# Splitting the two layer-norm loops of a transformer-layer kernel into halves one tile apart

## The chip, the cores and the metric

The kernel is one launch on the 8 cores of a Trainium2 chip. Every core runs the same program on its own data and no core waits for another. The metric is the device time of the slowest core, in microseconds (us). Each core has a matrix engine (TensorE, PE in the profile), a vector engine (VectorE, DVE), an activation engine (ScalarE, ACT), a general engine (GpSimd, POOL) and SyncE (SP). SP and POOL here mostly issue DMA transfers. Each engine works through its own instructions in order, and semaphores tie the engines together.

## The reference, cut to what matters

The input x has the shape (4, 2048, 2048). One layer is an attention block and a feed-forward block, each ahead of it a layer norm over the last axis and each added to its input:

```python
def _layernorm(x, axis=-1, eps=1e-5):
    m = jnp.mean(x, axis=axis, keepdims=True)
    v = jnp.var(x, axis=axis, keepdims=True)
    return (x - m) / jnp.sqrt(v + eps)

x = x + attn(_layernorm(x), ...)   # latent K/V, rotary part, 16 heads, causal, output projection
x = x + ffn(_layernorm(x), ...)    # silu(x gate * s) * (x up * s), then down * s; fp8 weights
```

Only the two `_layernorm` calls and the transposes behind them are touched by the change.

## The kernel before, in words

Two cores share one of the four sequences; each has all 2048 rows of it for keys and values and is answerable for 1024 rows of output. The stages follow one another, each closed by `kb.barrier()`, which makes every engine wait for all semaphores: first layer norm, latent projection, Q projection, attention in two groups of 8 heads, output projection with the residual written to the scratch tensor `res_scr`, second layer norm, gate and up, down.

The first layer norm runs over 16 tiles of 128 rows by 2048 values, the second over 8. Both have the same form. SP loads tile `it` (1 MB, float32) into `XT[it % 2]`, one half of the buffer `F32A`; there are two such halves. The load of tile `it` waits on SP until `lnct[it - 2]`, the normalisation of the tile that was in that half. Then `ln_tile` does the following. ACT sums the row (L242). DVE squares it and sums the squares (`scalar_tensor_tensor`, L244). Four DVE instructions on one column each make mean and variance (L247 to L250). ACT takes the square root (L252). DVE takes the reciprocal (L256) and writes the normalised tile in bf16 into `XHB` (L257). `vedge` is a DVE instruction followed by DVE's own wait for it, since the next instruction reads its result. The small values stand in `STAT`, 8 columns, used anew by every tile.

PE then transposes the 16 blocks of 128 by 128 in two halves (`tp_group`, L191), and DVE copies each half from PSUM into `BIG0` or `BIG1` (L197). The order on DVE is therefore: squares and small instructions of a tile, its reciprocal and normalisation, its two copies, and then the next tile. The order on ACT is: sum of a tile, its square root, sum of the next tile. The order is written out by hand: every engine's list is filled as the Python loops emit it.

The x load is L264, its wait comes two lines before it; the load of the second layer norm is L687. Behind the first stage POOL issues the load of the weights `wkvaT` (L208), behind the second that of `gatew` and `upw` (L721, L723).

Of the kernel before, what the change touches and what calls it, by code (L numbers as in the profile page):

```python
# [9 lines left out]
F32 = mybir.dt.float32  # L10
BF16 = mybir.dt.bfloat16
FP8 = mybir.dt.float8e4
AFT = mybir.ActivationFunctionType
# [80 lines left out]
def build_nc():  # L94
# [34 lines left out]
    res_d = nc.dram_tensor("res_scr", [1024, 2048], F32, kind="Internal")  # L129
# [4 lines left out]
    sb = lambda n, sh, dt: es.enter_context(nc.sbuf_tensor(n, sh, dt))  # L134
    pt = lambda n, sh, dt: es.enter_context(nc.psum_tensor(n, sh, dt))

    BIG0 = sb("BIG0", [128, 32768], BF16)
    BIG1 = sb("BIG1", [128, 16384], BF16)
    BIG2 = sb("BIG2", [128, 16384], BF16)
    LATT = sb("LATT", [128, 8192], BF16)  # L140
    XHB = sb("XHB", [128, 4096], BF16)
    WT = sb("WT", [128, 4096], BF16)
    PB = sb("PB", [128, 1024], BF16)
    SQB = sb("SQB", [128, 2048], BF16)
# [21 lines left out]
    BIASC = sb("BIASC", [128, 32], F32)  # L166
    BNS = sb("BNS", [128, 24], F32)
    AGG = sb("AGG", [128, 16], F32)
    STAT = sb("STAT", [128, 8], F32)
    KC = sb("KC", [128, 16], F32)  # L170
    MAXQ = sb("MAXQ", [128, 1], F32)
    MAXK = sb("MAXK", [128, 1], F32)
# [4 lines left out]
    EPSC = sb("EPSC", [128, 2], F32)  # L177

    PS = [pt(f"PS{i}", [128, 512], F32) for i in range(6)]
    PT = [pt("PT0", [128, 1024], BF16), pt("PT1", [128, 1024], BF16)]  # L180

    kb = KB(nc)
# [3 lines left out]
    A = bass.AP  # L186

    def tp_group(src, n, pti, dst, src_f32=False):
        kb.wait("tensor", "sV", kb.pt_ev[pti])
        for j in range(n):  # L190
            tct = kb.op("tensor", lambda e, j=j: e.matmul(  # L191
                PT[pti][:, j * 128:(j + 1) * 128], src[:, j * 128:(j + 1) * 128], IDB[:, :],
                is_transpose=True, start=(j == 0), stop=(j == n - 1)),
                inc="sT" if j == n - 1 else None)
        kb.wait("vector", "sT", tct)
        out_ap, in_ap = dst(n)
        ev = kb.op("vector", lambda e, o=out_ap, i=in_ap: e.tensor_copy(o, i), inc="sV")  # L197
        kb.pt_ev[pti] = ev
        return ev
# [11 lines left out]
    try:  # L211
# [4 lines left out]
        for dst0, src0 in consts:  # L216
            cload = kb.dma("sync", lambda e, d=dst0, s=src0: e.dma_start(
                out=d[:, :], in_=s.ap()[:, :]))
# [15 lines left out]
        XT = [F32A[:, 0:2048], F32A[:, 2048:4096]]  # L234

        def vedge(fn):
            v = kb.op("vector", fn, inc="sV")
            kb.wait("vector", "sV", v)
            return v

        def ln_tile(buf, xh, eps_col):
            s_sum = kb.op("scalar", lambda e, buf=buf: e.activation(  # L242
                BIG2[:, 0:2048], buf, AFT.Identity, accum_out=STAT[:, 0:1]), inc="sS")
            vedge(lambda e, buf=buf: e.scalar_tensor_tensor(  # L244
                SQB[:, 0:2048], buf, 1.0, buf, Op.mult, Op.mult, accum_out=STAT[:, 1:2]))
            kb.wait("vector", "sS", s_sum)
            vedge(lambda e: e.tensor_scalar(STAT[:, 2:3], STAT[:, 0:1], 1.0 / 2048, None, Op.mult))  # L247
            vedge(lambda e: e.tensor_scalar(STAT[:, 4:5], STAT[:, 1:2], 1.0 / 2048, None, Op.mult))
            vedge(lambda e: e.tensor_mul(STAT[:, 3:4], STAT[:, 2:3], STAT[:, 2:3]))
            v_var = kb.op("vector", lambda e: e.tensor_sub(STAT[:, 5:6], STAT[:, 4:5], STAT[:, 3:4]), inc="sV")  # L250
            kb.wait("scalar", "sV", v_var)
            s_sd = kb.op("scalar", lambda e, eps_col=eps_col: e.activation(  # L252
                STAT[:, 6:7], STAT[:, 5:6], AFT.Sqrt, bias=EPSC[:, eps_col:eps_col + 1],
                scale=1.0), inc="sS")
            kb.wait("vector", "sS", s_sd)
            vedge(lambda e: e.reciprocal(STAT[:, 7:8], STAT[:, 6:7]))  # L256
            return kb.op("vector", lambda e, xh=xh, buf=buf: e.tensor_scalar(  # L257
                xh, buf, STAT[:, 2:3], STAT[:, 7:8], Op.subtract, Op.mult), inc="sV")

        lnct, evA = {}, {}  # L260
        for it in range(16):
            if it >= 2:
                kb.wait("sync", "sV", lnct[it - 2])
            ld = kb.dma("sync", lambda e, it=it: e.dma_start(  # L264
                out=XT[it % 2], in_=xb.ap()[it * 128:(it + 1) * 128, :]))
            kb.wait("vector", *ld)
            kb.wait("scalar", *ld)
            xh = XHB[:, (it % 2) * 2048:(it % 2) * 2048 + 2048]
            if it >= 2:
                kb.wait("vector", "sT", evA[it - 2])  # L270
            lnct[it] = ln_tile(XT[it % 2], xh, 0)
            kb.wait("tensor", "sV", lnct[it])
            for half in range(2):
                src = xh[:, half * 1024:half * 1024 + 1024]
                dst = lambda n, half=half, it=it, pti=half: (
                    A(BIG0, half * 8 * 2048 + it * 128, [[32768, 128], [2048, 8], [1, 128]]),
                    PT[half][:, 0:1024])
                evA[it] = tp_group(src, 8, half, dst)
            evA[it] = kb.cnt["sT"]
        kb.barrier()  # L280

        cut(2)
# [20 lines left out]
        for dl in range(4):  # L303
# [5 lines left out]
            for tb in range(4):  # L309
# [26 lines left out]
                if pending is not None:  # L336
# [5 lines left out]
                                                      bias=EPSC[:, 1:2], scale=1.0 / 512), inc="sS")  # L342
# [66 lines left out]
        for hg in range(2):  # L409
            k_ev = {}  # L410
            mm_k = {}
            for i8 in range(8):
# [7 lines left out]
                for tb in range(4):  # L420
                    for c in range(4):
# [4 lines left out]
                            inc="sT" if (tb == 3 and c == 3) else None)  # L426
# [8 lines left out]
            for i8 in range(8):  # L435
# [37 lines left out]
                out=A(XHB, 0, [[4096, 128], [1024, 4], [1, 1024]]), in_=vin))  # L473
            kb.wait("tensor", *wv_ld)
            v_ev = {}
            for tt in range(16):
# [3 lines left out]
                for dl in range(4):  # L480
                    for ovb in range(2):
# [4 lines left out]
                            inc="sT" if (dl == 3 and ovb == 1) else None)  # L486
# [9 lines left out]
            for i8 in range(8):  # L496
                h = hg * 8 + i8
                for qb in range(2):
# [26 lines left out]
                    for j, kt in enumerate(slots):  # L525
# [12 lines left out]
                        elif pair_idx > 0:  # L538
# [4 lines left out]
                            bias=BIASC[:, qb * 16 + kt:qb * 16 + kt + 1],  # L543
# [22 lines left out]
                    if (pair_idx - 1) in wr_by:  # L566
# [5 lines left out]
                        out=lrow_d.ap()[hg * 16 + pgl:hg * 16 + pgl + 1, :], in_=LINV[0:1, 0:512]))  # L572
# [10 lines left out]
            out=F32A[0:32, 0:512], in_=lrow_d.ap()[0:32, :]))  # L583
# [5 lines left out]
            out=linv_d.ap()[0:32, :], in_=F32A[0:32, 512:1024]))  # L589
# [3 lines left out]
        for ch in range(4):  # L593
            srcb = A(linv_d, ch * 8 * 512, [[0, 128], [512, 8], [1, 512]])
            if ch >= 1 and last_n is not None:
                kb.wait("gpsimd", "sV", last_n)
            bc = kb.dma("gpsimd", lambda e, srcb=srcb: e.dma_start(
                out=F32A[:, 0:4096], in_=srcb, allow_slow_non_contiguous=True))
# [45 lines left out]
        for dt in range(16):  # L644
# [3 lines left out]
            for qb in range(2):  # L648
# [22 lines left out]
                if prev_add:  # L671
                    kb.wait("sync", "sV", prev_add[1])
                ld_blk = kb.dma("sync", lambda e, xin=xin, xsl=xsl: e.dma_start(
                    out=F32A[:, xsl * 512:xsl * 512 + 512], in_=xin))
# [5 lines left out]

        cut(9)
        kb.wait_all_dma("sync")
        ln2ct, evG = {}, {}
        for it in range(8):
            if it >= 2:
                kb.wait("sync", "sV", ln2ct[it - 2])
            ld = kb.dma("sync", lambda e, it=it: e.dma_start(  # L687
                out=XT[it % 2], in_=res_d.ap()[it * 128:(it + 1) * 128, :]))
            kb.wait("vector", *ld)
            kb.wait("scalar", *ld)  # L690
            xh = XHB[:, (it % 2) * 2048:(it % 2) * 2048 + 2048]
            if it >= 2:
                kb.wait("vector", "sT", evG[it - 2])
            ln2ct[it] = ln_tile(XT[it % 2], xh, 0)
            kb.wait("tensor", "sV", ln2ct[it])
            for half in range(2):
                src = xh[:, half * 1024:half * 1024 + 1024]
                dst = lambda n, half=half, it=it: (
                    A(BIG1, half * 8 * 1024 + it * 128, [[16384, 128], [1024, 8], [1, 128]]),
                    PT[half][:, 0:1024])  # L700
                tp_group(src, 8, half, dst)
            evG[it] = kb.cnt["sT"]
        kb.barrier()

        cut(10)
# [9 lines left out]
        for io in range(48):  # L715
            bufp = io % 2
            if io >= 2:
# [4 lines left out]
                out=W8[:, bufp * 2048:bufp * 2048 + 2048], in_=gin))  # L722
            g2 = kb.dma("gpsimd", lambda e, uin=uin, bufp=bufp: e.dma_start(  # L723
                out=W8[:, 4096 + bufp * 2048:4096 + bufp * 2048 + 2048], in_=uin))
# [37 lines left out]
        for dt in range(16):  # L762
            lds = {}
            for t3 in range(3):
                L = dt * 3 + t3
                slot = L % 4
                if L >= 4:
# [5 lines left out]
                    out=W8[:, slot * 2048:slot * 2048 + 2048], in_=din_ap)))  # L773
            for qb in range(2):
# [4 lines left out]
                for t3 in range(3):  # L779
                    slot, ld3 = lds[t3]  # L780
                    kb.wait("tensor", *ld3)
                    for cc in range(16):
# [6 lines left out]
                            inc="sT" if cc == 15 else None)  # L789
# [10 lines left out]
                if prev_ev:  # L800
                    kb.wait("sync", "sV", prev_ev)
                ld_blk = kb.dma("sync", lambda e, rin=rin: e.dma_start(
                    out=F32A[:, 3072:3584], in_=rin))
# [3 lines left out]
                for tq in range(4):  # L807
# [3 lines left out]
                        inc="sT" if tq == 3 else None)  # L811
# [3 lines left out]
                if prev_store[0]:  # L815
# [6 lines left out]
                    out=oout, in_=F32A[:, 3584:4096]))  # L822
# [83 lines left out]
```

How the kernel before makes its waits and increments, by code:

```python
        def w(e, fn=fn, h=h, n=n):  # L67
            fn(e).then_inc(h, n)
# [4 lines left out]
    def wait(self, eng, name, v):  # L73
        if v is None or v <= 0:
            return
        key = (eng, name)
        if self.lastwait.get(key, 0) >= v:
            return
        self.lastwait[key] = v
        h = self.semh[name]
        self.ops[eng].append(lambda e, h=h, v=v: e.wait_ge(h, v))
```

## Time and profile before

| | us |
|---|---|
| median of 3 runs | 2776.1 |
| lowest and highest of the 3 | 2657.79 and 2872.64 |
| the profiled execution | 2657.38 |
| its span on the slowest core (core 1) | 2655.8 |

The profile is one execution, on its slowest core. PE is busy for 70% of the span, ACT 24%, DVE 20%, POOL 9%. Times in a timeline count from the start of the span. A time between instructions is read as the difference of two starts; "busy" is the length of an instruction. DMA issues have the engine SPq or POOLq, and their "landing" is the time from the issue to the arrival of the last data.

### The profile page before, as it was taken

How to read it: one execution, taken by the hardware profiler on the slowest of the kernel's cores; microseconds unless marked ns; L12 is line 12 of the kernel's file. 1: busy time of each engine (PE TensorE's matmuls, PEld its weight loads, DVE VectorE, ACT ScalarE, POOL GpSimd, SP SyncE). 2: the span in 40 equal slices, each digit the busy share in tenths (PEclk: the TensorE clock that was granted, in tenths of full speed). 3: DMA queues.
4: the chain of work that ended last, by engine and by line, in shares of the span. 5: the costliest groups of instructions: out<-in, count | busy, mean ns of one | idle time of the engine just before them, and what ended most of it. 6: DMA issues, size and time to landing. Idle time of an engine off the chain costs nothing.

```text
span 2655.8 us, 24291 instructions; the slowest of 8 cores (2634.7 to 2655.8 us)
## 1 busy us (share of the span) xinstructions
PE 1859.9 (70%) x8614; PEld 796.2 (30%) x8614; DVE 518.8 (20%) x1045; ACT 636.7 (24%) x913; POOL 238.7 (9%) x241
## 2 busy tenths in 40 slices
PE   1268954676755766347734888888888887899998
PEld 1133422211122111023312333333333333344443
DVE  4620024144432344321142000000000000000000
ACT  2222200476712677301121111111111111000000
POOL 0000100000000000011001111111111111111110
PEclk9998978799987999778956999999999999999999
DMA  4334721000010000178845665666666654987895
GB/s 122 127 45 43 72 21 12 16 1 1 1 16 16 1 1 1 66 139 136 138 141 40 31 30 30 31 32 32 32 32 32 31 30 24 72 74 77 76 79 64
DMA packets 455719, 130.45 MB, mean 49 GB/s; under 512 B 385073, under 2 KB 450802, under 8 KB 452018
## 3 DMA queue, kind: packets, MB, share of 16 engines
q0 software_dynamic: 382720, 69.29, 39.3%
q1 hardware_dynamic: 72882, 59.61, 7.6%
q8 instruction: 72, 1.18, 0.2%
q14 instruction: 45, 0.37, 0.0%
HBM read 248.28 MB, written 16.91 MB: 100 GB/s over the span
## 4 chain that ended last, share of the span: by engine, by line
PE 59%; DVE 14%; DMA 11%; issue 7%; ACT 7%; DVEq 1%; ACTq 0%; SPq 0%; POOL 0%; POOLq 0%
PE PS L733 13%; PE PS L786 13%; PE PS L738 13%; DMA res_scr<-F32A 5%; PE PS L519 3%; ACT PB L541 3%; PE PS L362 3%; PE PS L422 3%; ACT PB L750 3%; DVE SQB L559 2%; PE PS L482 2%; PE PS L316 2%; PE PS L512 2%; DVE SQB L244 2%; DMA WT<-wqT 2%
## 5 line engine op out<-in xcount | busy, mean ns | idle before, releaser
L733 PE MATMUL PS<-BIG,W 128*128 128x512 bf16 x1536 | 349.8, 381 | 154.8 <-DVE BIG L754 139.0
L738 PE MATMUL PS<-BIG,W 128*128 128x512 bf16 x1536 | 347.2, 379 | 0.0
L786 PE MATMUL PS<-BIG,W 128*128 128x512 bf16 x1536 | 338.7, 380 | 11.1 <-DMA W<-downw 11.1
L733 PEld LDWEIGHTS PS<-BIG,W 128*128 128x128 fp8e4 x1536 | 144.0, 98 | 360.4 <-issue 203.0
L786 PEld LDWEIGHTS PS<-BIG,W 128*128 128x128 fp8e4 x1536 | 150.7, 98 | 187.1 <-issue 14.1
L738 PEld LDWEIGHTS PS<-BIG,W 128*128 128x128 fp8e4 x1536 | 150.2, 98 | 181.3
L754 DVE TENSOR_TENSOR BIG<-PB 128x512 bf16<-128x512 bf16 x96 | 40.8, 425 | 795.8 <-ACT PB L750 795.8
L541 ACT ACTIVATE PB<-PS,BIASC,SCL 128x512 bf16<-128x512 f32 x224 | 162.5, 776 | 125.1 <-PE PS L530 124.9
L656 PE MATMUL PS<-BIG,WT 128*128 128x512 bf16 x512 | 128.3, 409 | 67.3 <-DVE BIG L603 65.2
L512 PE MATMUL PS<-SQB,ONESCb 128*1 128x512 bf16 x224 | 86.7, 387 | 115.6 <-DVE SQB L559 115.4
L747 ACT ACTIVATE PB<-PS,GSCc 128x512 bf16<-128x512 f32 x96 | 66.1, 689 | 422.3 <-PE PS L733 422.3
L541 ACT ACTIVATE SQB<-PS,BIASC,SCL 128x512 bf16<-128x512 f32 x224 | 162.4, 778 | 7.6 <-PE PS L530 7.5
L191 PE MATMUL PT<-IDB,XHB 128*128 128x128 bf16 x384 | 44.8, 310 | 168.3 <-DVE XHB L257 168.3
L530 PE MATMUL PS<-BIG 128*128 128x512 bf16 x448 | 137.8, 390 | 24.7 <-ACT PB L541 21.5
L750 ACT ACTIVATE PB<-PS,USCc 128x512 bf16<-128x512 f32 x96 | 66.1, 689 | 258.6 <-PE PS L738 258.6
L362 PE MATMUL PS<-BIG,WT 128*128 128x512 bf16 x512 | 115.3, 385 | 16.1 <-DMA WT<-wqT 15.8
L721 POOL DMA_DIRECT2D W<-gatew x48 | 54.8, 1142 | 795.6 <-PE PS L738 693.4
L796 ACT ACTIVATE F32A<-PS,DSCc 128x512 f32<-128x512 f32 x32 | 22.1, 689 | 374.4 <-PE PS L786 374.4
L422 PE MATMUL PS<-LATT,WT 128*128 128x512 bf16 x256 | 69.7, 434 | 53.8 <-DVE BIG L430 38.3
L817 DVE TENSOR_TENSOR F32A<-PS,F32A 128x512 f32<-128x512 f32 x32 | 22.1, 692 | 375.6 <-PE PS L808 375.6
L656 PEld LDWEIGHTS PS<-BIG,WT 128*128 128x128 bf16 x512 | 53.4, 105 | 131.2 <-issue 85.0
L191 PEld LDWEIGHTS PT<-IDB,XHB 128*128 128x128 bf16 x384 | 39.1, 145 | 173.8 <-issue 173.8
(99 smaller groups left out, 1405.9 us busy)
## 6 DMA issues: line engine op xcount, KB each, us to landing
F32A<-xb SPq DMA_DIRECT2D x16, 1024.0 KB, 5.9
W<-gatew POOLq DMA_DIRECT2D x48, 256.0 KB, 7.1
W<-upw POOLq DMA_DIRECT2D x48, 256.0 KB, 8.8
W<-downw POOLq DMA_DIRECT2D x48, 256.0 KB, 7.1
WT<-wqT POOLq DMA_DIRECT2D x16, 512.0 KB, 6.7
F32A<-linv_scr POOLq DMA_DIRECT2D x4, 2048.0 KB, 7.9
WT<-outwT POOLq DMA_DIRECT2D x16, 512.0 KB, 9.3
F32A<-xb SPq DMA_DIRECT2D x32, 256.0 KB, 5.2
```

What stands on the lines that cost most here:

```text
L191: tct = kb.op("tensor", lambda e, j=j: e.matmul(PT[pti][:, j * 128:(j + 1) * 128], src[:, j * 128:(j + 1) * 128], IDB[:, :], is_transpose= ...
L362: mmct = kb.op("tensor", lambda e, c=c, pi=pi, ot=ot, qb=qb: e.matmul(PS[pi][:, :], WT[:, (ot % 2) * 2048 + c * 128:(ot % 2) * 2048 + (c + ...
L422: mmct = kb.op("tensor", lambda e, c=c, tb=tb, i8=i8: e.matmul(PS[tb][:, :], WT[:, (i8 % 2) * 2048 + c * 128:(i8 % 2) * 2048 + (c + 1) * 128],
L512: kb.op("tensor", lambda e, p=p, isf=(p == 0), isl=(p == npair - 1): e.matmul(PS[5][0:1, 0:512], ONESCb[:, 0:1], PADD[p % 2], start=isf, s ...
L519: isf=(i == 0), isl=(i == nsl - 1), po=po: e.matmul(PS[po][:, :], BIG0[:, VOFF + kt_i * 1024 + i8 * 128:VOFF + kt_i * 1024 + i8 * 128 + 12 ...
L530: t_s = kb.op("tensor", lambda e, sb_=sb_, i8=i8, kt=kt, qb=qb, h=h: e.matmul(sb_[:, :], BIG0[:, KOFF + i8 * 2048 + kt * 128:KOFF + i8 * 2 ...
L541: exp_by[(pair_idx, j)] = kb.op("scalar", lambda e, pi=pi, sb_=sb_, qb=qb, kt=kt: e.activation(PSL4[pi], sb_[:, :], AFT.Exp, bias=BIASC[:, ...
L656: mmct = kb.op("tensor", lambda e, c=c, pi=pi, dt=dt, qb=qb: e.matmul(PS[pi][:, :], WT[:, (dt % 2) * 2048 + c * 128:(dt % 2) * 2048 + (c + ...
L733: mmg = kb.op("tensor", lambda e, c=c, qb=qb, bufp=bufp: e.matmul(PS[0][:, :], W8[:, bufp * 2048 + c * 128:bufp * 2048 + (c + 1) * 128], B ...
L738: mmu = kb.op("tensor", lambda e, c=c, qb=qb, bufp=bufp: e.matmul(PS[1][:, :], W8[:, 4096 + bufp * 2048 + c * 128:4096 + bufp * 2048 + (c ...
L750: s_up = kb.op("scalar", lambda e, io=io: e.activation(PB[:, 512:1024], PS[1][:, :], AFT.Identity, scale=USCc[:, io:io + 1]), inc="sS")
L786: isl=(t3 == 2 and cc == 15): e.matmul(PS[pi][:, :], W8[:, slot * 2048 + cc * 128:slot * 2048 + (cc + 1) * 128], fuse_ap(c, qb), start=isf ...
```

## The change

`ln_tile` is cut into `ln_half1` (sum, squares, the four small instructions, square root) and `ln_half2` (reciprocal and normalisation). A turn `it` of each loop now emits the load of tile `it`, `ln_half1` of tile `it`, and then `ln_half2`, transposes and copies of tile `it - 1`; the last tile's second part stands behind the loop. `STAT` grows to two sets of 8 columns. The two `XT` buffers, the two halves of `XHB`, the PSUM tiles and SP's wait for `lnct[it - 2]` stay as they are. The second loop is changed in the same way.

```diff
-    STAT = sb("STAT", [128, 8], F32)
+    STAT = sb("STAT", [128, 16], F32)
...
-        def ln_tile(buf, xh, eps_col):
+        def ln_half1(buf, par, eps_col):
+            ST = STAT[:, par * 8:par * 8 + 8]
...
             kb.wait("scalar", "sV", v_var)
-            s_sd = kb.op("scalar", lambda e, eps_col=eps_col: e.activation(
-                STAT[:, 6:7], STAT[:, 5:6], AFT.Sqrt, bias=EPSC[:, eps_col:eps_col + 1],
+            return kb.op("scalar", lambda e, eps_col=eps_col: e.activation(
+                ST[:, 6:7], ST[:, 5:6], AFT.Sqrt, bias=EPSC[:, eps_col:eps_col + 1],
                 scale=1.0), inc="sS")
-            kb.wait("vector", "sS", s_sd)
-            vedge(lambda e: e.reciprocal(STAT[:, 7:8], STAT[:, 6:7]))
+
+        def ln_half2(par, xh, buf, sdct):
+            ST = STAT[:, par * 8:par * 8 + 8]
+            kb.wait("vector", "sS", sdct)
+            vedge(lambda e: e.reciprocal(ST[:, 7:8], ST[:, 6:7]))
             return kb.op("vector", lambda e, xh=xh, buf=buf: e.tensor_scalar(
-                xh, buf, STAT[:, 2:3], STAT[:, 7:8], Op.subtract, Op.mult), inc="sV")
+                xh, buf, ST[:, 2:3], ST[:, 7:8], Op.subtract, Op.mult), inc="sV")
...
         for it in range(16):
             if it >= 2:
                 kb.wait("sync", "sV", lnct[it - 2])
...
             kb.wait("vector", *ld)
             kb.wait("scalar", *ld)
-            xh = XHB[:, (it % 2) * 2048:(it % 2) * 2048 + 2048]
-            if it >= 2:
-                kb.wait("vector", "sT", evA[it - 2])
-            lnct[it] = ln_tile(XT[it % 2], xh, 0)
-            kb.wait("tensor", "sV", lnct[it])
...
+            sdA[it] = ln_half1(XT[it % 2], it % 2, 0)
+            if it >= 1:
+                jt = it - 1
+                if jt >= 2:
+                    kb.wait("vector", "sT", evA[jt - 2])
+                xh = XHB[:, (jt % 2) * 2048:(jt % 2) * 2048 + 2048]
+                lnct[jt] = ln_half2(jt % 2, xh, XT[jt % 2], sdA[jt])
+                emit_tp(jt, xh, BIG0, 2048, 16)
+        jt = 15
+        kb.wait("vector", "sT", evA[jt - 2])
+        xh = XHB[:, (jt % 2) * 2048:(jt % 2) * 2048 + 2048]
+        lnct[jt] = ln_half2(jt % 2, xh, XT[jt % 2], sdA[jt])
+        emit_tp(jt, xh, BIG0, 2048, 16)
         kb.barrier()
```

`emit_tp` holds the transposes and copies that stood in the loop, unchanged; the second loop has `emit_tpG` for the same.

## Rows read from the trace of the kernel before

**Rows 1.** Page, shares of the chain that ended last, by engine

```profile
PE 59%; DVE 14%; DMA 11%; issue 7%; ACT 7%; DVEq 1%; ACTq 0%; SPq 0%; POOL 0%; POOLq 0%
```

**Rows 2.** Spans by core (span, mean granted TensorE clock)

```profile
core 0: 2643.9 us, clock 0.931
core 1: 2655.8 us, clock 0.929
core 4: 2653.0 us, clock 0.930
```

**Rows 3.** Waits, core 1, 36 to 152 us (total us, times, longest)

```profile
PE PT L191 <- DVE XHB L257: 89.5, 14, 6.6
DVE BIG L197 <- PE PT L191: 21.2, 29, 1.3
DVE STAT L256 <- ACT STAT L252: 6.9, 14, 0.5
```

**Rows 4.** Timeline, core 1, one tile of the first layer norm (start, length, [idle before])

```profile
66.13 1.35 DVE L257 TENSOR_SCALAR XHB<-F32A,STAT 128x2048 bf16<-128x2048 f32 x1
67.60 0.33 SPq L264 DMA_DIRECT2D F32A<-xb  x1
...
69.59 0.69 DVE L197 COPY BIG<-PT 128x1024 bf16<-128x1024 bf16 x1 [0.16 <-PE PT L191]
70.20 2.28 DVE L244 SCALAR_TENSOR_TENSOR SQB<-F32A 128x2048 bf16<-128x2048 f32 x1
...
73.44 0.16 DVE L250 TENSOR_TENSOR STAT<-STAT 128x1 f32<-128x1 f32 x1
73.70 0.30 ACT L252 ACTIVATE STAT<-STAT,EPSC 128x1 f32<-128x1 f32 x1 [6.05 <-DVE STAT L250]
73.90 1.90 ACT L242 ACTIVATE BIG<-F32A 128x2048 bf16<-128x2048 f32 x1
74.09 0.16 DVE L256 RECIPROCAL STAT<-STAT 128x1 f32<-128x1 f32 x1 [0.49 <-ACT STAT L252]
74.36 1.35 DVE L257 TENSOR_SCALAR XHB<-F32A,STAT 128x2048 bf16<-128x2048 f32 x1
```

**Rows 5.** Line L264, the x loads on core 1: time to landing

```profile
DMA to landing us min/median/max: 5.6/5.9/7.3
```

**Rows 6.** Core 0: an x load in the timeline, and line L264's landing

```profile
66.99 0.33 SPq L264 DMA_DIRECT2D F32A<-xb  x1
DMA to landing us min/median/max: 4.7/4.9/7.0
```

**Rows 7.** Core 5, then core 4: an x load, and line L264's landing

```profile
65.19 0.33 SPq L264 DMA_DIRECT2D F32A<-xb  x1
DMA to landing us min/median/max: 4.9/5.0/6.0
67.88 0.33 SPq L264 DMA_DIRECT2D F32A<-xb  x1
DMA to landing us min/median/max: 4.7/4.9/7.5
```

**Rows 8.** Line L687, second layer norm: first issues and landing, core 1

```profile
1345.07 0.81 SPq L687 DMA_DIRECT2D F32A<-res_scr  x2
DMA to landing us min/median/max: 4.8/4.8/6.9
```

**Rows 9.** The same, first issues of cores 0, 2 and 3, and core 3's landing

```profile
1339.32 0.81 SPq L687 DMA_DIRECT2D F32A<-res_scr  x2
1329.66 12.79 SPq L687 DMA_DIRECT2D F32A<-res_scr  x3
1338.80 0.81 SPq L687 DMA_DIRECT2D F32A<-res_scr  x2
DMA to landing us min/median/max: 4.8/5.8/6.9
```

**Rows 10.** Timeline, core 1: start and end of the first layer norm

```profile
19.83 2.29 DVE L244 SCALAR_TENSOR_TENSOR SQB<-F32A 128x2048 bf16<-128x2048 f32 x1 [3.19 <-DMA F32A<-xb]
23.98 0.16 DVE L250 TENSOR_TENSOR STAT<-STAT 128x1 f32<-128x1 f32 x1
...
152.23 0.69 DVE L197 COPY BIG<-PT 128x1024 bf16<-128x1024 bf16 x1 [0.16 <-PE PT L191]
```

**Rows 11.** Timeline, core 1: start and end of the second layer norm

```profile
1349.98 2.29 DVE L244 SCALAR_TENSOR_TENSOR SQB<-F32A 128x2048 bf16<-128x2048 f32 x1 [7.60 <-DMA F32A<-res_scr]
...
1353.47 1.28 ACT L252 ACT_TABLE_LOAD   x1 [1.50 <-DVE STAT L250]
1355.79 1.35 DVE L257 TENSOR_SCALAR XHB<-F32A,STAT 128x2048 bf16<-128x2048 f32 x1
...
1416.95 0.69 DVE L197 COPY BIG<-PT 128x1024 bf16<-128x1024 bf16 x1 [0.16 <-PE PT L191]
```

More of the change, by code:

```diff
@@ L239, in vedge @@
             return v
-        def ln_tile(buf, xh, eps_col):
+        def ln_half1(buf, par, eps_col):
+            ST = STAT[:, par * 8:par * 8 + 8]
             s_sum = kb.op("scalar", lambda e, buf=buf: e.activation(
-                BIG2[:, 0:2048], buf, AFT.Identity, accum_out=STAT[:, 0:1]), inc="sS")
+                BIG2[:, 0:2048], buf, AFT.Identity, accum_out=ST[:, 0:1]), inc="sS")
             vedge(lambda e, buf=buf: e.scalar_tensor_tensor(
-                SQB[:, 0:2048], buf, 1.0, buf, Op.mult, Op.mult, accum_out=STAT[:, 1:2]))
+                SQB[:, 0:2048], buf, 1.0, buf, Op.mult, Op.mult, accum_out=ST[:, 1:2]))
@@ L246, in ln_tile @@
             kb.wait("vector", "sS", s_sum)
[L247 to L250, printed above, removed]
+            vedge(lambda e: e.tensor_scalar(ST[:, 2:3], ST[:, 0:1], 1.0 / 2048, None, Op.mult))
@@ L251, in ln_tile @@
+            vedge(lambda e: e.tensor_scalar(ST[:, 4:5], ST[:, 1:2], 1.0 / 2048, None, Op.mult))
+            vedge(lambda e: e.tensor_mul(ST[:, 3:4], ST[:, 2:3], ST[:, 2:3]))
+            v_var = kb.op("vector", lambda e: e.tensor_sub(ST[:, 5:6], ST[:, 4:5], ST[:, 3:4]), inc="sV")
             kb.wait("scalar", "sV", v_var)
-            s_sd = kb.op("scalar", lambda e, eps_col=eps_col: e.activation(
-                STAT[:, 6:7], STAT[:, 5:6], AFT.Sqrt, bias=EPSC[:, eps_col:eps_col + 1],
+            return kb.op("scalar", lambda e, eps_col=eps_col: e.activation(
+                ST[:, 6:7], ST[:, 5:6], AFT.Sqrt, bias=EPSC[:, eps_col:eps_col + 1],
@@ L260, in build_nc, with emit_tp @@
-        lnct, evA = {}, {}
+                xh, buf, ST[:, 2:3], ST[:, 7:8], Op.subtract, Op.mult), inc="sV")
+        lnct, evA, sdA = {}, {}, {}
+        def emit_tp(it, xh, big, width, nchunk):
+            kb.wait("tensor", "sV", lnct[it])
+            for half in range(2):
+                src = xh[:, half * 1024:half * 1024 + 1024]
+                dst = lambda n, half=half, it=it: (
+                    A(big, half * 8 * width + it * 128,
+                      [[nchunk * width, 128], [width, 8], [1, 128]]),
+                    PT[half][:, 0:1024])
+                tp_group(src, 8, half, dst)
+            evA[it] = kb.cnt["sT"]
@@ L267, in build_nc @@
             kb.wait("scalar", *ld)
-            xh = XHB[:, (it % 2) * 2048:(it % 2) * 2048 + 2048]
-            if it >= 2:
-                kb.wait("vector", "sT", evA[it - 2])
-            lnct[it] = ln_tile(XT[it % 2], xh, 0)
-            kb.wait("tensor", "sV", lnct[it])
[L273 to L279, printed above, removed]
+            sdA[it] = ln_half1(XT[it % 2], it % 2, 0)
[11 more added lines that the diff above has]
+        emit_tp(jt, xh, BIG0, 2048, 16)
         kb.barrier()
@@ L682, in build_nc, with emit_tpG @@
         kb.wait_all_dma("sync")
[L683 to L694, printed above, removed]
+        ln2ct, evG, sdG = {}, {}, {}
+        def emit_tpG(it, xh):
             kb.wait("tensor", "sV", ln2ct[it])
@@ L702, in build_nc @@
             evG[it] = kb.cnt["sT"]
+        for it in range(8):
+            if it >= 2:
+                kb.wait("sync", "sV", ln2ct[it - 2])
+            ld = kb.dma("sync", lambda e, it=it: e.dma_start(
+                out=XT[it % 2], in_=res_d.ap()[it * 128:(it + 1) * 128, :]))
+            kb.wait("vector", *ld)
+            kb.wait("scalar", *ld)
+            sdG[it] = ln_half1(XT[it % 2], it % 2, 0)
+            if it >= 1:
+                jt = it - 1
+                if jt >= 2:
+                    kb.wait("vector", "sT", evG[jt - 2])
+                xh = XHB[:, (jt % 2) * 2048:(jt % 2) * 2048 + 2048]
+                ln2ct[jt] = ln_half2(jt % 2, xh, XT[jt % 2], sdG[jt])
+                emit_tpG(jt, xh)
+        jt = 7
+        kb.wait("vector", "sT", evG[jt - 2])
+        xh = XHB[:, (jt % 2) * 2048:(jt % 2) * 2048 + 2048]
+        ln2ct[jt] = ln_half2(jt % 2, xh, XT[jt % 2], sdG[jt])
+        emit_tpG(jt, xh)
         kb.barrier()
```

## The prediction, made before the changed kernel ran

> **What bounds the kernel now.** I looked at the cores first [rows 2]. All have about the same clock, and core 1 ends last by 2.8 us; a core that starts 12 us earlier than another gives nothing, so the sum is made on core 1 and then held against its neighbours. The chain over the whole span is mostly PE [rows 1], but this says little here: a barrier closes each stage, so a layer-norm stage that grows by some time moves all behind it by that time. What counts is what ends last inside the two stages.
>
> The first stage runs from 19.83 to 152.92 us [rows 10], the second from 1349.98 to 1417.64 us [rows 11]. Among the waits of the first, none in the steady part is for a DMA; PE waits for DVE's normalisation, DVE waits for PE's transposes (29 times, 21.2 us) and for ACT's square root (14 times, 6.9 us) [rows 3]. So DVE is the ring that turns. The timeline of a tile gives the ring's parts, and one turn is 74.36 − 66.13 = 8.23 us [rows 4]:
> - normalisation, L257: 1.35 us;
> - from its end (67.48) to the end of the second copy (70.28): 2.80 us, with the 1.3 us that PE takes ahead of the first copy;
> - from the start of the squares (70.20) to the end of L250 (73.60): 3.40 us;
> - from there to the start of the reciprocal (74.09), over ACT and back: 0.49 us;
> - from the reciprocal to the start of the normalisation: 0.27 us.
>
> The loads are beside this ring. The load issued at 67.60, 0.12 us after the normalisation has freed its buffer, is for the tile after the next: its first reader is ACT's sum at 73.90, 6.3 us after the issue, and DVE squares it one turn after 70.20, at 78.43, 10.8 us after the issue. It lands in 5.9 us [rows 5]. It is hidden, but on ACT by 0.4 us only.
>
> **The change part by part.**
>
> *The square root off the ring.* DVE now has other work between L250 of a tile and that tile's reciprocal. Where DVE is not otherwise held up this takes away 0.49 us per tile and puts in its place the step from L250 to an instruction that needs nothing from it. No row has just that step. It is at least nothing, and at most the 0.11 us that DVE leaves where an instruction does wait for its predecessor (reciprocal's end at 74.25, normalisation at 74.36 [rows 4]). I take 0.07, nearer to the row. DVE alone would then need 8.23 − 0.42 = 7.81 us per tile.
>
> *The normalisation moved behind the next tile's first half.* No instruction is added; PE's transposes, their two copies and their PSUM tiles keep their places behind it. But SP's wait for `lnct[it − 2]` moves with it, and this is the one that pays. The load of tile k+2 still needs the normalisation of tile k, since there are two buffers. Before, DVE copied tile k and did the first half of tile k+1, its reciprocal, its normalisation and its copies before it read tile k+2. Now the first half of k+1 is already done; after the normalisation of k come its two copies (2.80 us), and the very next DVE instruction is the squares of k+2. So the load has 2.80 us of cover in place of 10.8, and what is late next is DVE itself, on the load. Behind the waiting squares stand, in DVE's order, the reciprocal and normalisation of k+1, and for these wait PE and SP's next load; the loop is closed. ACT's sum of k+2 waits for the same load and runs beside the squares (1.90 against 2.28 us), so it adds nothing, and the square root has a whole turn of time.
>
> The new ring is: normalisation's end to the issue 0.12, landing L, squares to the end of L250 3.40, the step 0.07, reciprocal to normalisation 0.27, normalisation 1.35; together 5.21 + L, and the wake-up after landing, which I read from the second stage: issue 1345.07 to squares 1349.98 is 4.91 us where the landing is 4.8 [rows 8, 11]. I use 4.91 for a load that is not disturbed: a turn of 10.12 us, against 8.23, so 1.89 us more.
>
> *Which L.* Core 1 has 5.9 us and core 0 4.9 us [rows 5, 6]. I read these as pairs. Core 1 issues 0.61 us after core 0 (67.60 and 66.99) and is the one with the long landing. Cores 5 and 4 are 2.7 us apart, and their medians are 5.0 and 4.9 [rows 7]. In the second stage core 1 issues 5.75 us after core 0 and now has 4.8 us; core 3 stands 9.14 us behind core 2, one turn and 0.9 us, and has 5.8 [rows 8, 9]. So the extra 1.0 us belongs to a load issued some tenths of a microsecond after the neighbour's, not to the core. Before, DVE kept the pair at the same distance. In the new ring the load's time is part of the turn, so the later core falls back by 1.0 us a turn until it is clear of the neighbour, which from 0.6 to at least 2.7 us takes 2 to 3 turns: about 2.5 us in all, once.
>
> *First stage, core 1.* The first two loads are issued together ahead, as before. The squares of tile 1 now follow L250 of tile 0 (24.14), start at about 24.21, and their L250 ends at 27.61; reciprocal at 27.68, first normalisation 27.95 to 29.30. Then 14 turns wait for a load: 29.30 + 14 × 10.12 = 170.98. Behind this come the copies of tile 14 (2.80), reciprocal and normalisation of tile 15 (0.05 + 1.62) and its copies (2.80): 178.3 us against 152.9, **+25.3**, and with the pair's falling apart **+27.8**.
>
> *Second stage.* The same, with 6 such turns. Its first square root needs a table load of 1.28 us [rows 11], which DVE used to wait for. Now it lies beside the squares of tile 1, but ACT's sum of tile 1 is behind it: square root to 1355.07, sum 1354.97 to 1357.06, L247 to L250 of tile 1 until 1358.05, normalisation of tile 0 until 1359.7 (before, 1357.14). The second load was issued 0.5 us after the first and even at the largest landing, 6.9 [rows 8], is there at 1352.5, ahead of its squares at 1353.5. Then 6 × 10.12 = 60.7 and 7.27 as above: 1427.7 against 1417.6, **+10.1**.
>
> PE behind the stages starts on weights whose load POOL issues after the barrier, as before; nothing there moves. The wider `STAT` costs nothing: each instruction still has one column.
>
> *The sum.* 2657.4 + 27.8 + 10.1 = **2695.3 us**, 1.4% more. It stands against the profiled execution (2657.38, about the lowest of the runs, 2657.79); the median shown, 2776.1, is of runs that went otherwise and isn't the base here.
>
> DMA: Bandwidth & Descriptors, section Anatomy of one DMA, of the Trainium skill fits about 2.0 us plus the bytes at 436 GB/s, for transfers issued by GpSimd; that makes an estimate of 4.4 us for 1 MB where the rows, issued by SP, have 4.8 to 5.9. By it the turn would be 0.5 us shorter and the sum 10 us less, 2685; the measured landings decide.
>
> **The rivals.**
> - *The long landing stays* (the pair does not fall apart, or both cores slow each other now that neither has slack): 14 × 1.07 + 6 × 1.0 − 2.5 = 18.5 us more, 2713.8. For it: 5.9 is core 1's median of 16 loads [rows 5]. Against it: rows 8 give core 1 4.8 once the distance is large. Worse still, if a load took the 7.3 us of the largest [rows 5], a turn is 12.6 and the time 2657.4 + 35.4 + 20 × 2.5, about 2743; but that value is of the two loads issued together at the start.
> - *The load is hidden after all*, the side of faster or no change. It decides at a landing below 2.80 − 0.12 − 0.1 = 2.6 us: then every turn is 7.81, 22 tiles save 0.42 each, and the time is about 2648. Nothing speaks for it; no 1 MB load of the cores in these rows lands under 4.7 us. The Trainium skill, in Trainium Kernel Development and Optimization under Best Practices, asks for double buffers to overlap DMA with compute; counted in buffers both kernels obey it, and then this rival's time would follow. The rows show why the count does not do: what matters is the time from a buffer's being freed to its being read, which falls from 10.8 to 2.8 us.
> - *Part of the ring is shorter than I read*: if the fast landing is 4.7 everywhere, the step after L250 nothing and the falling apart free, it is 20 × 0.2 + 20 × 0.07 + 2.5 = 8 us less, 2687. The other stages are the same program on other data, and the cores' spans differ by 12 us [rows 2]; some of that can move either way and takes this case down to about 2678.
>
> **How the numbers follow.** The forecast case, the landing near 4.9 after a short fight, has 0.66 (2686 to 2704). The long landing staying has 0.17 (2705 to 2725), something longer 0.04, the shorter ring 0.10 (2678 to 2686), the hidden load 0.03. The range 2680 to 2716 leaves out the hidden load, the lowest edge of the shorter ring and the upper part of the long landings. Slower by over 2%, about what a measurement of this kernel can tell from no change, begins at 2710.5: part of the second and all of the third case, 0.14. Within 2%: 0.85. Faster by over 2%: 0.01.
>
> **What the profile of the changed kernel would show.** DVE's squares L244 idle ahead of each tile from the third on, released by the DMA of `xb` or `res_scr`, by about 2.2 us (0.12 + 4.91 − 2.80); starts of successive normalisations 10.1 us apart; no idle of the reciprocal on ACT; landings of 4.8 to 4.9 on both cores of each pair after the first turns, with the later core's distance grown to over 1.5 us. A first stage ending near 181 us on core 1 and a second that is 78 us long confirm the sum. Idle of 3.3 us ahead of L244 would be the long landing; turns of 7.8 us and no idle would refute the whole. The forecast is wrong, too, if a stage that the diff doesn't touch changes by more than a few microseconds.

## The result and the profile after

| | before | changed |
|---|---|---|
| median of 10 runs, us | 2677.29 | 2697.03 |
| lowest, us | 2652.97 | 2691.77 |
| profiled execution, us | 2657.38 | 2704.25 |
| its longest span, us | 2655.8 (core 1) | 2702.7 (core 5) |

The change makes the kernel slower: the ratio is 1.0139, with a 95% interval of 1.0124 to 1.0154. Both medians contain runs in which the cores of a die had a lower clock; the ratio compares the others.

The kernel is easiest to read in five pieces. "First" and "second" are the two layer norms, each from the start of its first squares to the end of its last copy; "head", "middle" and "tail" are what lies around them. These are differences of starts in the timelines (for core 1 of before the ends are in [rows 10, 11]).

| us | head | first | middle | second | tail |
|---|---|---|---|---|---|
| before, core 1 | 19.8 | 133.1 | 1197.1 | 67.7 | 1238.2 |
| before, all cores | 17.4 to 20.1 | 133.0 to 133.1 | 1182.9 to 1197.1 | 67.6 to 67.7 | 1231.8 to 1238.9 |
| changed, core 1 | 19.8 | 161.1 | 1189.1 | 76.6 | 1235.4 |
| changed, all cores | 17.9 to 20.0 | 159.2 to 164.1 | 1185.4 to 1211.0 | 76.1 to 78.3 | 1230.4 to 1237.1 |

Both touched stages are longer on every core, and the tail is not. In the mean over the eight cores the first stage grew by 27.7 us and the second by 9.0. The middle differs by 14 us between cores already in one execution of before, so single spans say less than the two stages do.

Two groups of DVE on core 1 of the changed kernel: the squares, L245 (L244 of before), and the reciprocal, L260 (L256 of before). After the first bar stand the busy time in us and the mean of one in ns, after the second the idle time just before them and what ended it:

```profile
L245 DVE SCALAR_TENSOR_TENSOR SQB<-F32A 128x2048 bf16<-128x2048 f32 x24 | 55.0, 2293 | 58.3 <-DMA F32A<-xb 37.3 <-DMA F32A<-res_scr 20.9
L260 DVE RECIPROCAL STAT<-STAT 128x1 f32<-128x1 f32 x24 | 3.7, 156 | 0.0
```

The same two groups on core 1 of the kernel before:

```profile
L244 DVE SCALAR_TENSOR_TENSOR SQB<-F32A 128x2048 bf16<-128x2048 f32 x24 | 54.8, 2283 | 10.8 <-DMA F32A<-res_scr 7.6 <-DMA F32A<-xb 3.2
L256 DVE RECIPROCAL STAT<-STAT 128x1 f32<-128x1 f32 x24 | 3.9, 164 | 13.5 <-ACT STAT L252 13.5
```

The squares are as long as before. DVE stands idle ahead of them for 58.3 us in all, each time until a load arrives; before it was 10.8 us, all of it at the first tile of the two stages ([rows 10, 11]). The reciprocal is the change's own aim, and it is met: it waited 13.5 us for ACT and no longer waits. The waits of core 1 from 36 to 152 us (total, times, longest), to be held against [rows 3], where no DMA occurs:

```profile
PE PT L191 <- DVE XHB L261: 92.6, 11, 9.1
ACT BIG L243 <- DMA F32A<-xb: 76.8, 12, 7.1
DVE SQB L245 <- DMA F32A<-xb: 29.3, 12, 3.2
DVE BIG L197 <- PE PT L191: 15.7, 22, 1.3
```

One turn in the timeline of core 1 (start, length), to be held against [rows 4]:

```profile
58.63 1.35 DVE L261 TENSOR_SCALAR XHB<-F32A,STAT 128x2048 bf16<-128x2048 f32 x1
60.10 0.33 SPq L280 DMA_DIRECT2D F32A<-xb  x1
62.09 0.69 DVE L197 COPY BIG<-PT 128x1024 bf16<-128x1024 bf16 x1 [0.16 <-PE PT L191]
65.02 2.29 DVE L245 SCALAR_TENSOR_TENSOR SQB<-F32A 128x2048 bf16<-128x2048 f32 x1 [2.23 <-DMA F32A<-xb]
68.28 0.16 DVE L251 TENSOR_TENSOR STAT<-STAT 128x1 f32<-128x1 f32 x1
68.35 0.16 DVE L260 RECIPROCAL STAT<-STAT 128x1 f32<-128x1 f32 x1
68.62 1.35 DVE L261 TENSOR_SCALAR XHB<-F32A,STAT 128x2048 bf16<-128x2048 f32 x1
```

From one normalisation to the next it is 9.99 us, 8.23 before. The load goes out at 60.10, behind the normalisation that frees its buffer; the copies end at 62.78; then DVE has nothing until 65.02. From the issue to the squares it is 4.92 us.

### The profile page after: what moved, and what is told of

Read it like the earlier page. It is cut to its first block, busy times and chain, and to the rows that moved or that the text cites. A ratio compares the mean times of both kernels' runs of the same rounds, so it can differ in the third digit from the quotient of the medians.

```text
span 2702.7 us, 24269 instructions; the slowest of 8 cores (2669.9 to 2702.7 us)
## 1 busy us (share of the span) xinstructions
PE 1864.8 (69%) x8614; PEld 797.8 (30%) x8614; DVE 518.5 (19%) x1045; ACT 639.0 (24%) x913; POOL 238.9 (9%) x241
## 4 chain that ended last, share of the span: by engine, by line
PE 56%; DMA 15%; DVE 14%; issue 7%; ACT 7%; DVEq 1%; SPq 0%; ACTq 0%; POOL 0%; POOLq 0%
PE PS L762 13%; PE PS L815 12%; PE PS L767 12%; DMA res_scr<-F32A 5%; PE PS L536 3%; DMA F32A<-xb 3%; ACT PB L558 3%; PE PS L439 3%; ACT PB L779 2%; PE PS L379 2%; DMA WT<-wqT 2%; PE PS L499 2%; PE PS L529 2%; DVE SQB L576 2%; PE PS L333 2%
```

## The experiments

My theory (A) is that of the forecast: the skewed order (a tile's second half done one tile later) holds each buffer longer, so that its load has only the two copies, 2.80 us, to hide behind and stands in DVE's ring. The main rival (B) is that the new order itself, or the work that now runs side by side, costs the time.

**A third buffer, in either order.** First, the changed kernel with a third tile buffer:

```diff
+        NB = 3
+        XA = (XT + [BIG1[:, 0:4096].bitcast(F32), BIG1[:, 4096:8192].bitcast(F32)])[:NB]
+        XG = (XT + [BIG2[:, 4096:8192].bitcast(F32), BIG2[:, 8192:12288].bitcast(F32)])[:NB]
...
-            if it >= 2:
-                kb.wait("sync", "sV", lnct[it - 2])
+            if it >= NB:
+                kb.wait("sync", "sV", lnct[it - NB])
...
```

The loads and both halves of a tile then use `XA[it % NB]`, in the second layer norm `XG[it % NB]`.

> The changed kernel with a third tile buffer in each layer norm (laid over BIG1 in the first, over BIG2 in the second), so a load waits for the normalisation three tiles back and not two. Theory A (the held buffer is the whole loss): a load has one more turn of cover, DVE no longer idles ahead of its squares L245, and a turn is DVE's own work, 3.34 + 0.26 + 1.35 + 2.72 = 7.7 us. First layer norm about 127 us (133.1 before, 159 to 164 changed), second about 66 us (67.7, 76 to 78), whole kernel 6 to 8 us under the kernel before, ratio about 0.997. Theory B (the skewed order itself costs DVE or ACT time): turns stay at 9 to 10 us, stages near 160 and 76, ratio about 1.01.

Measured: first layer norm 124.7 us and second 62.7, the same on all eight cores. The ratio to before is 0.9951 (95% interval 0.9935 to 0.9967, as in the brackets below), the lowest run 2640.41 us. Its timeline on core 1, with idle times in brackets where there are any:

```profile
59.90 2.28 DVE L248 SCALAR_TENSOR_TENSOR SQB<-F32A 128x2048 bf16<-128x2048 f32 x1
63.22 0.15 DVE L263 RECIPROCAL STAT<-STAT 128x1 f32<-128x1 f32 x1
63.48 1.34 DVE L264 TENSOR_SCALAR XHB<-BIG,STAT 128x2048 bf16<-128x2048 f32 x1
66.94 0.69 DVE L197 COPY BIG<-PT 128x1024 bf16<-128x1024 bf16 x1 [0.16 <-PE PT L191]
67.55 2.28 DVE L248 SCALAR_TENSOR_TENSOR SQB<-F32A 128x2048 bf16<-128x2048 f32 x1
```

The squares have no idle time ahead of them; a turn is 67.55 − 59.90 = 7.65 us. So the skewed order does gain, 0.6 us a tile against 8.23, and the whole loss comes from the buffer that it holds. The stages came out 2 to 3 us under what I expected. I had counted a full turn for the last tile, which has only its second half: its normalisation follows the one before by 4.7 us.

Then the third buffer in the kernel before, in its serial order, the same edit there:

> The kernel before, in its serial order, with the third tile buffer in each layer norm. Theory A (in the kernel before the load is hidden, and only the skewed order needs the third buffer): no change, stages of 133.1 and 67.7 us, ratio 1.000 within 0.003. Rival (the third buffer is itself what gained 11 us in the three-buffer version of the changed kernel): stages near 125 and 63, ratio 0.995.

Measured: 133.1 and 67.7 us on all eight cores, not moved by 0.1 us. The lowest run was 2655.21 us; no ratio is on record for it, so this rests on the stages. The third buffer is worth nothing by itself.

**The late load without the skew.**

```diff
             if it >= 2:
-                kb.wait("sync", "sV", lnct[it - 2])
+                kb.wait("sync", "sV", lnct[it - 1])
```

The second layer norm has the same edit.

> The kernel before in its serial order; only SP's wait is moved: the load of tile it waits for the normalisation of tile it-1 instead of it-2. Theory A: the load stands in the ring without any skew; a turn is 0.12 + 4.91 + 3.40 + 0.49 + 0.27 + 1.35 = 10.5 us; first layer norm 133.1 + 14 x 2.3 = 165 us, second 67.7 + 6 x 2.3 = 81.6 us, whole about +46 us. Theory B (the order, not the load's time of issue, costs): stages stay at 133 and 68.

Measured: 167.9 to 170.2 us and 81.4 to 84.2 us; the profiled execution's longest span is 2701.1 us, 45.3 more than that of before. Waits on core 1, 36 to 150 us (total, times, longest):

```profile
ACT BIG L242 <- DMA F32A<-xb: 76.4, 11, 7.4
DVE SQB L244 <- DMA F32A<-xb: 26.4, 11, 2.9
DVE STAT L256 <- ACT STAT L252: 4.9, 10, 0.5
```

The order of the work is that of before, the reciprocal's wait for ACT is there, and the same loss appears. The time of the load's issue alone makes it. This kernel is slower than the changed one on every core, by 4.5 to 9.8 us in the first stage and by 3.3 to 8.0 in the second. It keeps the wait for ACT's square root, 0.49 us a tile, that the skew does save.

**The load's length.** The changed kernel, but from the third tile on a load brings only 1024 of the 2048 columns:

```diff
-                out=XT[it % 2], in_=xb.ap()[it * 128:(it + 1) * 128, :]))
+                out=XT[it % 2][:, 0:(2048 if it < 2 else 1024)], in_=xb.ap()[it * 128:(it + 1) * 128, 0:(2048 if it < 2 else 1024)]))
```

The second layer norm has the same edit.

> The changed kernel, but every tile's load from the third on brings only its first 1024 columns (512 KB in place of 1 MB); the rest of the buffer keeps old data, so this part of the computation is left out. Theory A: the turn follows the load's time one for one. At the 400 GB/s seen while a load runs, 512 KB less is 1.3 us, so a turn falls from 10.0 to about 8.7 us; DVE's idle ahead of its squares from 2.3 to about 1.0 us; first layer norm about 141 us, second about 68.5. Theory B (a fixed cost of the hand-over, not the bytes): turns stay near 10.0.

Measured: 142.9 to 144.3 us and 69.0 to 72.8 us, in one run of 2674.19 us. From the issue to the squares it was mostly 3.7 to 3.9 us instead of 4.9 to 5.1. DVE's squares on core 1 in the first layer norm, first of this kernel, then of the changed one:

```profile
L245 DVE SCALAR_TENSOR_TENSOR SQB<-F32A 128x2048 bf16<-128x2048 f32 x16 | 36.7, 2292 | 19.8 <-DMA F32A<-xb 19.6
```

```profile
L245 DVE SCALAR_TENSOR_TENSOR SQB<-F32A 128x2048 bf16<-128x2048 f32 x16 | 36.7, 2292 | 37.3 <-DMA F32A<-xb 37.3
```

Idle falls by 17.5 us over 14 loads, 1.25 us each; the stage on core 1 by 17.5 us too (161.1 to 143.6). The turn follows the load one for one. It also shows that half the bytes are not half the time: 1.2 us less out of 4.9 for 512 KB less out of 1 MB.

**What the gain of a lighter DVE is worth.** In both kernels DVE is the busiest engine of these stages and ACT has slack: on core 1 of before, from 36 to 152 us, DVE is busy for 80.5 us and ACT for 29.0. A version with the skewed order, four tile buffers, the two PSUM copies on ACT, and ACT's sum put a tile ahead of them (cuts of its edit against the changed kernel):

```diff
-    STAT = sb("STAT", [128, 16], F32)
+    STAT = sb("STAT", [128, 32], F32)
...
-        kb.wait("tensor", "sV", kb.pt_ev[pti])
+        kb.wait("tensor", "sS", kb.pt_ev[pti])
...
-        kb.wait("vector", "sT", tct)
+        kb.wait("scalar", "sT", tct)
-        ev = kb.op("vector", lambda e, o=out_ap, i=in_ap: e.tensor_copy(o, i), inc="sV")
+        ev = kb.op("scalar", lambda e, o=out_ap, i=in_ap: e.activation(o, i, AFT.Identity), inc="sS")
...
+        NB = 4
...
+                sdA[it] = ln_half1(XA[it % NB], it % 4, 0, sums[it])
+                if it + 1 < 16:
+                    ld_sum(it + 1)
```

`ld_sum(it + 1)` is ACT's sum of the next tile; it stands ahead of the copies of tile `it - 1`.

> A version meant to beat both: changed order, four tile buffers in each layer norm, ACT's sum issued a tile ahead, and both PSUM copies of a tile moved from DVE to ACT. Theory A (with the load out of the ring, the busiest engine sets the turn): DVE needs 3.34 + 0.26 + 1.35 + 0.1 = 5.1 us a tile; ACT 2.1 + 0.3 + two copies at about 1.1 with gaps, 5.0 to 5.6. First layer norm about 94 us, second about 51, whole 50 to 60 us under the kernel before, ratio near 0.98. Rival: 1 MB in every 5.3 us on all cores at once is more than the loads bear; landings grow and the turn is 6 to 7 us, ratio about 0.985 to 0.99; DVE then idles on the load.

Measured: 83.7 us on all cores and 44.4 (44.6 on one core). The ratio is 0.971 (0.969 to 0.9729), the lowest run 2579.04 us. Timeline on core 1:

```profile
60.93 2.28 DVE L251 SCALAR_TENSOR_TENSOR SQB<-F32A 128x2048 bf16<-128x2048 f32 x1
62.37 1.94 ACT L197 ACTIVATE BIG<-PT 128x1024 bf16<-128x1024 bf16 x2 [0.64 <-PE PT L191]
64.55 1.34 DVE L268 TENSOR_SCALAR XHB<-F32A,STAT 128x2048 bf16<-128x2048 f32 x1
64.63 1.90 ACT L246 ACTIVATE BIG<-BIG 128x2048 bf16<-128x2048 f32 x1
65.81 2.28 DVE L251 SCALAR_TENSOR_TENSOR SQB<-BIG 128x2048 bf16<-128x2048 f32 x1
```

A turn is 4.88 us, and on core 1 no engine waits for a load once the first tiles are in. The two stages together give 72.7 us, where I expected 56: the turn was taken as 5.3 us, with gaps on ACT that are not there (a copy takes 0.97 us, not 1.1), and the last tile was again counted as a full turn. The rival, loads that grow when each core asks for 1 MB every 4.9 us, did not come about. The medians of landing in the first stage were 4.9 to 5.8 us over the cores, where before has 4.8 to 5.9.

The same kernel with two buffers in place of four (`NB = 2`, and the sum emitted behind the next load):

> The version with the skewed order and the copies on ACT, but with two tile buffers in place of four (ACT's sum still ahead of its copies). Theory A: the load stands in the ring again and DVE's lighter turn cannot be used; a turn is 5.1 + 4.9 = 10.0 us, first layer norm about 157 to 160 us (83.7 with four buffers), second about 75 (44.4). All of the gain goes, whole kernel about 30 us over the kernel before. Rival (ACT's copies bring the gain whatever the loads do): stages stay near 84 and 44.

Measured: 157.5 to 159.8 us and 74.8 to 77.8 us, longest span of the profiled execution 2686.5 us. Squares on core 1 in the first layer norm:

```profile
L251 DVE SCALAR_TENSOR_TENSOR SQB<-F32A 128x2048 bf16<-128x2048 f32 x16 | 36.7, 2293 | 74.4 <-DMA F32A<-xb 74.4
```

DVE is rid of the two copies and of the waits for PE ahead of them, 2.8 us per tile in the changed kernel, and a turn is still about 10 us. What DVE gave up has become its idle time, 74.4 us in place of 37.3. This is the clearest sign of what bounds the skewed order with two buffers.

**The copies alone, in the old order.** The kernel before with only the three lines of `tp_group` that move the copies to ACT, the first three pairs of lines behind `STAT` in the edit above:

> The kernel before with nothing changed but the two PSUM copies of a tile done by ACT. ACT's sum of the next tile now stands behind these copies in ACT's order. Theory A (an engine's order decides, not its busy time): normalisation's end to first copy 1.2, copies 1.9, sum 2.1, then four small instructions, square root, reciprocal, normalisation 3.1: a turn of about 8.4 us, stages near 136 and 69, no gain. Rival (DVE's 2.8 us of copies come off the turn): 5.5 us a turn, stages near 93 and 50.

Measured: 135.6 to 135.7 us and 68.7 to 68.8 us, in one run of 2663.73 us. Timeline on core 1:

```profile
86.09 1.94 ACT L197 ACTIVATE BIG<-PT 128x1024 bf16<-128x1024 bf16 x2 [3.08 <-PE PT L191]
87.92 1.91 ACT L242 ACTIVATE BIG<-F32A 128x2048 bf16<-128x2048 f32 x1
90.02 0.15 DVE L247 TENSOR_SCALAR STAT<-STAT 128x1 f32<-128x1 f32 x1 [3.08 <-ACT BIG L242]
```

ACT waits 3.08 us for PE with the next tile's sum standing behind that wait, its data long there; and then DVE waits 3.08 us for the sum. Moving work to a free engine gained nothing, since the piece that was not ready stood ahead of the one that was.

So the sum goes ahead of the copies, in serial order and with two buffers, which takes `STAT` of 16 columns as well:

> The kernel before with the copies on ACT and ACT's sum of the next tile put ahead of them; DVE's order stays serial and there are two tile buffers as before. Theory A: a load now has one turn of DVE, 5.5 us, of cover for its 4.9, just enough; a turn is 3.40 + 0.49 + 0.27 + 1.35 = 5.5 us, first layer norm about 93 us, second about 49, whole about 58 us under the kernel before, ratio near 0.978. Rival (the cover is too thin and pairs of cores disturb each other's loads): turns of 6 to 6.5 us with DVE idle on the load, first stage 100 us or more, ratio near 0.982.

Measured: 93.0 to 93.6 us and 48.5 to 51.3 us; ratio 0.979 (0.9774 to 0.9807). Timeline on core 1:

```profile
89.28 1.34 DVE L260 TENSOR_SCALAR XHB<-F32A,STAT 128x2048 bf16<-128x2048 f32 x1
90.40 1.91 ACT L242 ACTIVATE BIG<-F32A 128x2048 bf16<-128x2048 f32 x1 [1.49 <-DMA F32A<-xb]
90.55 2.28 DVE L247 SCALAR_TENSOR_TENSOR SQB<-F32A 128x2048 bf16<-128x2048 f32 x1
```

Here ACT, which waits for the load, starts at 90.40, 0.15 us ahead of the squares that need the same tile: hidden, and just so. In the second stage it sometimes isn't, and the spread of 48.5 to 51.3 goes with that. This version needs no further tile buffer and has most of the gain; skew and two more buffers add 0.8% of the kernel.

## Why the prediction was right, and where it was wrong

- **The mechanism held.** DVE's idle on the load, its place ahead of the squares, and the vanished wait of the reciprocal are as forecast: 2.23 us of idle in the turn shown, 2.2 forecast; a turn of 9.99 us there, where 10.12 was forecast. The third buffer, the late load in the old order and the half load each moved the stages by nearly what the theory says.
- **The stages.** First layer norm on core 1: 133.1 to 161.1, +28.0, with +27.8 forecast. Second: 67.7 to 76.6, +8.9, with +10.1 forecast. Together 36.9 us on 2655.8, 1.39%; the forecast was 37.9.
- **The step that failed: what the sum was held against.** The forecast calls 2% "about what a measurement of this kernel can tell from no change" and puts 0.85 on "within 2%". No row gave that figure, and it is the wrong one: the measured interval is 0.15% to either side, so 1.0139 is a plain loss. "Within 2%" hid what the sum itself, +1.4%, had already said. The time was also put on a base of its own. It stands on the profiled execution, 2657.38 us, and sets the shown median of 2776.1 aside. Held against 2776.1 the number 2695.3 would read as a gain of 3%, which no step of the working says. The ten runs of before have since given a median of 2677.29, with five of them from 2652.97 to 2663.09, so the base itself was sound; what was missing is the change said as a ratio to it, and how finely such a ratio can be measured.
- **The stages that the diff does not touch were put at nothing.** The forecast says that nothing moves there, and lets the scatter between cores in only for its shorter case. On core 1 the middle is 8.0 us shorter than before and the tail 2.8 shorter, so core 1's span grew by 26.2 us only, to 2682.0, where a sum made on core 1 says 37.9. The profiled execution took 2704.25 us on core 5, whose middle was 1211.0. That the forecast time, 2695.3, lies 1.7 us from the median of the ten runs is therefore luck in part. The forecast had named a change of such a stage by more than a few microseconds as a sign of its being wrong; the sign was badly chosen. In the kernel with a third buffer and the old order, whose two layer norms are those of before to 0.1 us, the middle of core 1 is 1187.5 us, 9.5 shorter than before. Why the middle moves is open.
- **Terms of the first stage that were mis-sized and cancel, on core 1.** From a load's issue to its squares the forecast has 4.91 us; the 14 loads took 5.15 in the mean, 3.3 us more in all. The step from L251 to the reciprocal was taken as 0.07 us after the end; the reciprocal starts 0.09 us before it (68.35 against 68.28 + 0.16 = 68.44), 0.16 us less a turn, 2.2 us in all and 1 us in the second stage. The 2.5 us for the pair's falling apart were not due on core 1, which stood 1.9 us behind core 0 at its first ring load already. Three small delays had no term, 1.1 us together; the next point but one shows two of them.
- **The pair.** The falling apart is seen on other cores. Core 5, only 0.2 us behind core 4 in this execution, took turns of 11.23, 10.93 and 10.94, and then 10.17 us; core 3, 0.7 us behind core 2, one of 11.48 and then 10.28. Issues of cores 4 and 5 in the timelines, in each pair of rows core 4 first, and after two of them the start of core 5's sum:

```profile
28.51 0.33 SPq L280 DMA_DIRECT2D F32A<-xb  x1
...
28.73 0.33 SPq L280 DMA_DIRECT2D F32A<-xb  x1
34.45 1.91 ACT L243 ACTIVATE BIG<-F32A 128x2048 bf16<-128x2048 f32 x1 [7.00 <-DMA F32A<-xb]
...
49.62 0.33 SPq L280 DMA_DIRECT2D F32A<-xb  x1
...
50.88 0.33 SPq L280 DMA_DIRECT2D F32A<-xb  x1
56.73 1.91 ACT L243 ACTIVATE BIG<-F32A 128x2048 bf16<-128x2048 f32 x1 [7.12 <-DMA F32A<-xb]
...
59.62 0.33 SPq L280 DMA_DIRECT2D F32A<-xb  x1
...
61.82 0.33 SPq L280 DMA_DIRECT2D F32A<-xb  x1
```

  Core 5 is 0.22, 1.26 and 2.20 us behind, and its loads take 5.7, 5.85 and then 5.1 us to the squares. So the mechanism goes as forecast, on other cores than the one I put it on. That it is the neighbour's load which delays is read from many such distances; no run put the pair's distance on purpose, and it stays an inference.
- **Four long turns on core 1 had no term.** Four of its later turns took 10.4 to 10.9 us. Two have a late load (see the last section). The other two have loads of the usual length, but a delay beside them: in one the instruction behind the squares starts 2.83 us after them and not 2.48, in the other SP issues the last load 0.55 us after the normalisation's end and not 0.12:

```profile
106.28 2.29 DVE L245 SCALAR_TENSOR_TENSOR SQB<-F32A 128x2048 bf16<-128x2048 f32 x1 [2.30 <-DMA F32A<-xb]
109.11 0.15 DVE L248 TENSOR_SCALAR STAT<-STAT 128x1 f32<-128x1 f32 x1 [0.53 <-DVE SQB L245]
...
161.61 1.35 DVE L261 TENSOR_SCALAR XHB<-F32A,STAT 128x2048 bf16<-128x2048 f32 x1
163.51 0.33 SPq L280 DMA_DIRECT2D F32A<-xb  x1
```

  All eight cores have both delays, each at the same tile. What causes them is not known.

The advice to double-buffer that the forecast took from the Trainium skill (Trainium Kernel Development and Optimization, Best Practices) is met in number by the changed kernel and by the two-buffer version with ACT's copies, and both are slower than the kernel before. As the runs have it, what counts is how long a buffer has been free when its next content is wanted, for a load of 4.9 us: about 11 us in the kernel before, 2.8 in the changed one, 10.5 there with a third buffer, and about 5.4 in the serial version with the sum ahead. For the estimate by the Trainium skill's DMA: Bandwidth & Descriptors, section Anatomy of one DMA, the two sizes can now be compared: its slope gives an estimate of 1.2 us for 512 KB, and the runs show 1.2; its sum of 4.4 us for 1 MB is 0.5 under the 4.9 that stands here between issue and use.

## What to carry to other kernels

Before a loop is skewed, write down for each buffer when it is freed and when its next content is wanted; a skew by one tile takes a turn from that distance, and the number of buffers has to grow with it. Read that distance in the trace as the time from the instruction that frees to the first that reads, and compare it with issue to landing; if it is shorter, work taken off the busy engine only becomes idle time on it. When work moves to a free engine, look at what then stands behind its waits: here the same move was worth nothing, 2.1% or 2.9%, by order and buffers alone.

## What the runs showed of the hardware that was not expected

Two loads on each core in the first stage take 0.4 to 1.5 us longer than their neighbours, from issue to squares, in the changed kernel, in the one with the late load and in the one with half loads, whatever their distance to the other core. On core 0 of the changed kernel the load issued at 87.81 is one. DMA queues of core 0 in two stretches of 6 and 7 us with one load each, 77 to 83 us and then 87 to 94 us (packets, MB, share of 16 engines):

```profile
q1 hardware_dynamic: 144, 1.05, 52.6%
```

```profile
q1 hardware_dynamic: 144, 1.05, 43.6%
q8 instruction: 1, 0.02, 1.4%
```

The second stretch holds a packet of the instruction queue, and that load lands in 5.4 us, the first in 4.9. The other long load of core 0, issued at 148.87, has such a packet too. In the kernel before these packets are there as well, and nothing waits for the loads beside them. The view calls the queue one of instructions; that fetching the program's own code is what delays these loads fits, but was not tried. A packet of this kind is not enough by itself: on core 0 the last load, issued at 159.76, has one of another such queue (q14, 0.01 MB) beside it and lands in 4.9 us, and it is so on all eight cores (4.8 to 5.0).

Two ACT copies of 128 by 1024 bf16 out of PSUM in a row take 1.94 us, 0.97 each, against 0.69 us each on DVE. And a DVE instruction that does not wait for its predecessor begins about 0.09 us before that one's recorded end (68.35 against 68.44), where one that waits begins 0.11 after it (the normalisation at 68.62 against the reciprocal's end at 68.51).
